# Turning the feed-forward rows by transposing transfers, widened by ScalarE, in place of TensorE transposes

## The reference, cut to what matters

```python
def _rmsnorm(x, g):
    return g * (x * rsqrt(mean(x * x, -1) + EPS))
def _act_quant(x):
    scale = 127.0 / clip(max(abs(x), -1), 0.0001)
    return clip(round(x * scale), -128, 127) / scale
def _linear_bit(x, w, g):
    return einsum('bsd,od->bso', _act_quant(_rmsnorm(x, g)), _ternary_quant(w))
h = silu(_linear_bit(x, w1, g1)) * _linear_bit(x, w2, g2)      # 512 -> 2048
ffn = _linear_bit(h, w3, g3)                                    # 2048 -> 512
...
x = x + tanh(g_xattn) * xattn(layernorm(x), ctx)
x = x + tanh(g_ffn) * ffn(layernorm(x))                         # x: 2 x 512 x 512
```

## Time and profile before

| what | value |
|---|---|
| time, median of 3 runs | 653.92 us (652.92 to 654.09) |
| the profiled execution's own time | 656.19 us |
| its span | 654.4 us |
| PE, DVE, ACT, POOL busy over the span | 97%, 82%, 65%, 55% |
| granted TensorE clock | full in every slice |
| the feed-forward steps t = 2 to 7 and the end | from about 570 us to the end |

### The profile page before, as it was taken

One profiled execution on the slowest core, in us unless ns is written; L12 is line 12 of the kernel. 1 busy time (PEld: TensorE's weight loads), 2 busy tenths in 40 slices (PEclk: granted clock), 3 DMA queues, 4 the chain that ended last, 5 costly groups with the idle time before them and its releaser, 6 DMA issues.

```text
span 654.4 us, 9986 instructions
## 1 busy us (share of the span) xinstructions
PE 635.1 (97%) x2968; PEld 394.0 (60%) x2968; DVE 536.5 (82%) x870; ACT 422.2 (65%) x693; POOL 360.2 (55%) x304
## 2 busy tenths in 40 slices
PE   8789999999999999999999999999999998999997
PEld 7555466766766676666666666566656554545553
DVE  4778787788878877887789978997899987998863
ACT  2564686477737764776567766776666633598875
POOL 4722376655545554565367854664457144686651
PEclk9999999999999999999999999999999999999999
DMA  8207976788589858984988798878689872000001
GB/s 283 87 6 188 274 196 164 206 223 240 151 227 241 219 131 239 251 224 106 251 222 221 201 242 224 222 195 231 169 221 251 198 177 81 1 1 33 17 35 48
DMA packets 45208, 112.79 MB, mean 172 GB/s; under 512 B 11888, under 2 KB 15088, under 8 KB 45040
## 3 DMA queue, kind: packets, MB, share of 16 engines
q1 hardware_dynamic: 42128, 104.24, 60.1%
q10 hardware_dynamic: 2976, 8.06, 4.0%
q0 software_dynamic: 64, 0.00, 0.0%
HBM read 45.16 MB, written 2.10 MB: 72 GB/s over the span
## 4 chain that ended last, share of the span: by engine, by line
PE 68%; DVE 10%; SPq 8%; ACT 4%; issue 4%; DMA 3%; POOL 1%; PEld 1%; POOLq 0%; ACTq 0%; DVEq 0%; PEldq 0%
PE ps_s L1443 11%; SPq L1132 8%; PE ps_b L1476 6%; PE ps_s L623 5%; PE ps_ctx L1476 5%; PE ps_b L1339 4%; PE ps_b L1394 4%; DMA G<-E 3%; PE ps_b L1341 3%; PE ps_b L1413 3%; PE ps_b L1340 3%; ACT E L1675 2%; PE ps_b L674 2%; DVE small L1858 2%; PE ps_ctx L1472 2%
## 5 line engine op out<-in xcount | busy, mean ns | idle before, releaser
L1675 ACT ACTIVATE E<-ps_s,small 128x1024 f32<-128x1024 f32 x128 | 142.5, 1116 | 143.4 <-DVE small L1858 110.5
L1241 POOL TENSOR_TENSOR G_lo<-G,g_hi 128x512 fp32r<-128x512 f32 x130 | 168.0, 1306 | 117.7 <-ACT g_hi L1619 117.7
L1858 DVE TENSOR_REDUCE small<-ps_s 128x1 f32<-128x1024 f32 x128 | 149.8, 1211 | 34.5 <-PE ps_s L1443 34.3
L1872 DVE STREAM_TRANSPOSE E<-E 128x1024 f32<-128x1024 f32 x124 | 152.0, 1230 | 0.1
L1199 POOL TENSOR_SCALAR E<-E,small 128x1024 f32<-128x1024 f32 x64 | 78.9, 1233 | 109.6 <-DVE small L1864 98.0
L1619 ACT ACTIVATE g_hi<-G 128x512 fp32r<-128x512 f32 x130 | 76.9, 631 | 3.5 <-DVE wq L1888 3.5
L1339 PE MATMUL ps_b<-b_hi,ctx_hi 128*128 128x512 f32 x128 | 66.8, 522 | 0.3 <-DVE ctx_lo L1818 0.3
L1476 PE MATMUL ps_b<-G,kv 128*128 128x512 f32 x126 | 63.7, 600 | 1.7 <-DMA G<-E 1.7
L1476 PE MATMUL ps_ctx<-G,kv 128*128 128x512 f32 x126 | 64.6, 607 | 0.1
L1443 PE MATMUL ps_s<-k_hi,q_hi 64*128 64x512 f32 x256 | 57.3, 444 | 3.8 <-ACT E L1675 2.6
L623 PE MATMUL ps_s<-wq,q12T 128*128 128x512 fp8e4 x256 | 59.8, 379 | 0.1
(11 more groups left out here) (203 smaller groups left out, 1211.7 us busy)
## 6 DMA issues: line engine op xcount, KB each, us to landing
G<-E SPq DMA_DIRECT2D x496, 128.0 KB, 2.6
w_stage<-in_wffn SPq DMA_DIRECT2D x37, 512.0 KB, 4.8
w_stage<-in_wffn ACTq DMA_DIRECT2D x11, 512.0 KB, 4.4
wo_s<-in_woT SPq DMA_DIRECT2D x8, 512.0 KB, 5.4
wq_s<-in_wq SPq DMA_DIRECT2D x7, 512.0 KB, 5.5
wkcq_s<-in_wkcqT SPq DMA_DIRECT2D x7, 384.0 KB, 3.4
out<-x_sb SPq DMA_DIRECT2D x8, 256.0 KB, 2.0
x_sb<-in_x SPq DMA_DIRECT2D x3, 512.0 KB, 6.3
```

The source lines that it names most:

```text
L1241: nc.gpsimd.tensor_tensor(g_tile(w % 2, i, G_lo), tile, high_part(i).bitcast(F32).rearrange("p (t i q) -> p t i q", t=ST, i=4), ALU.subtra ...
L1675: nc.scalar.activation(out, scores, ACT.Exp, bias=negmax[:, k:k + 1], accum_out=rowsum[:, k:k + 1]).then_inc(exp_done, 1)
L1858: nc.vector.tensor_reduce(negmax[:, k:k + 1], ps_s[:, t % 2, :], AX_X, ALU.max, negate=True).then_inc(max_done, 1)
L1872: nc.vector.transpose(e_tile(w % 2, t), e_tile(w % 2, t)).then_inc(blocks_turned, 1)
```

## The change

For the normed rows of tiles 2 to 7 and the hidden rows of tiles 0 to 5, TensorE's transposes and ScalarE's copies out of PSUM go. In their place ScalarE rewrites the rounded int16 rows as bf16 in the same bytes (`widen_rows`, 128 x 1024, and `widen_hidden`, 128 x 2048), and SP issues a transfer that turns them from SBUF to SBUF (`dma_start_transpose`), one for each. The first two tiles' rows and the last two tiles' hidden rows are turned by TensorE as before. Every wait on the old copies now waits for the transfer.

```diff
-        T3_AT = (1, 2)
+        FIRST_MOVED, LAST_MOVED = 2, 5
...
+            def turn_rows(t):
+                sp.wait_ge(q12_wide, t - FIRST_MOVED + 1)
+                sp.wait_ge(up_done, HC * (t - 1))
+                sp.dma_start_transpose(q12T[:, t % 2, :, :, :].rearrange("p i c s -> p (i c) s"),
+                                       qn12[:, t % 2, :, :].rearrange("p i d -> p (i d)").bitcast(BF16)).then_inc(q12_moved[t % 2], 16)
+
+            def turn_hidden(t):
+                sp.wait_ge(q3_wide, t + 1)
+                if t >= 2:
+                    sp.wait_ge(mm3_done, t - 1)
+                sp.dma_start_transpose(q3T[:, t % 2, :, :], qn3[:, t % 2, :].bitcast(BF16)).then_inc(q3_moved[t % 2], 16)
+
+            for t in range(1, TT):
+                if t + 1 < TT:
+                    turn_rows(t + 1)
+                if t >= 2:
+                    turn_hidden(t - 2)
+                if t >= 3:
+                    store(t - 3)
+            for t in range(LAST_MOVED, TT):
+                store(t)
...
         def gate_up(pe, t, k, c):
-            pe.wait_ge(q12T_ready, 2 if early and c == 1 else t + 1)
+            if t < FIRST_MOVED:
+                pe.wait_ge(q12T_ready, 2 if early and c == 1 else t + 1)
+            else:
+                pe.wait_ge(q12_moved[t % 2], 16 * (t // 2))
...
                     if out and not (isinstance(t, int) and t == LAST):
-                    pe.wait_ge(et_free, 2 * t + (ET_FREE0 - 2))
+                    pe.wait_ge(q3_moved[t % 2], 16 * (t // 2))
...
+        def widen_rows(act, t):
+            act.wait_ge(q12_ready, t + 1)
+            rows = qn12[:, t % 2, :, :].rearrange("p i d -> p (i d)")
+            copy_act(rows.bitcast(BF16), rows).then_inc(q12_wide, 1)
+
+        def widen_hidden(act, t):
+            act.wait_ge(q3_ready, t + 1)
+            rows = qn3[:, t % 2, :]
+            copy_act(rows.bitcast(BF16), rows).then_inc(q3_wide, 1)
...
                     if turn and c == 0:
-                        turned_rows(act, t, k)
-                    if out and c in T3_AT:
-                        a = T3_AT.index(c)
-                        act.wait_ge(t3_done, 2 * t + (a - 3))
-                        copy_act(q3T[:, k, 8 * a:8 * a + 8, :].rearrange("p c s -> p (c s)"), t3[:, a, :]).then_inc(et_free, 1)
+                        widen_rows(act, t + 1)
...
                 if t == 1:
                     silu(act, 2, 0, 0)
+                    widen_hidden(act, 0)
                     norm_act(act, 2, 0)
-                elif mm:
+                else:
+                    widen_hidden(act, t - 1)
                     hidden_square(act, t, k)
```

More of the change, by code:

```diff
@@ L464, in build @@
         atanh_pool, yg_first = sem("atanh_pool"), sem("yg_first")
+        q12_wide, q3_wide = sem("q12_wide"), sem("q3_wide")
+        q12_moved, q3_moved = [sem("q12_moved0"), sem("q12_moved1")], [sem("q3_moved0"), sem("q3_moved1")]
         mm3_done, side_read, stored, ffn_chain, atanh_dve, atanh_act, ln2_var, ln2_done, ln2_bias = (
@@ L528, in ffn_sp, with store @@
             sp.dma_start(g3, A["g3"].partition_broadcast(P)).then_inc(ld_g3, 16)
-            with sp.Fori(0, TT) as t:
+            def store(t):
                 sp.wait_ge(side_read, t + (SIDE_READ0 + 1))
-                sp.dma_start(out_dram[:, bass.ds(t, 1), :], x_sb[:, bass.ds(t, 1), :]).then_inc(stored, 16)
+                sp.dma_start(out_dram[:, t:t + 1, :], x_sb[:, t:t + 1, :]).then_inc(stored, 16)
+            def turn_rows(t):
[17 more added lines that the diff above has]
+                store(t)
             sp.wait_ge(stored, 16 * TT)
@@ L615, in gate_up @@
             cols = slice(c * NF, (c + 1) * NF)
-            early = isinstance(t, int) and t == 0
-            pe.wait_ge(q12T_ready, 2 if early and c == 1 else t + 1)
+            early = t == 0
+            if t < FIRST_MOVED:
+                pe.wait_ge(q12T_ready, 2 if early and c == 1 else t + 1)
+            else:
+                pe.wait_ge(q12_moved[t % 2], 16 * (t // 2))
             if not (early and c < 2):
@@ L658, in step @@
                             pe_last_out(pe, s)
-                    if turn and c == 0:
-                        turn_rows(pe, t, k)
-                    if out and c in T3_AT:
-                        a = T3_AT.index(c)
[L663 to L668, removed]
                 if out and not (isinstance(t, int) and t == LAST):
-                    pe.wait_ge(et_free, 2 * t + (ET_FREE0 - 2))
+                    pe.wait_ge(q3_moved[t % 2], 16 * (t // 2))
                     pe.wait_ge(side_read, t + (SIDE_READ0 - 2))
@@ L680, in turn_half @@
                 pe.wait_ge(q3_half, 2 * (t - (LAST - 1)) + a + 1)
-                pe.wait_ge(et_free, 2 * t + (a - 1 + ET_FREE0))
+                pe.wait_ge(et_free, ET_FREE0 + (a + 1 if t == LAST else 0))
                 for b in range(8):
@@ L687, in down_half @@
             def down_half(t, a):
-                pe.wait_ge(et_free, 2 * t + (a + 1 + ET_FREE0))
+                if t <= LAST_MOVED:
+                    pe.wait_ge(q3_moved[t % 2], 16 * (t // 2 + 1))
+                else:
+                    pe.wait_ge(et_free, 2 * (t - LAST_MOVED - 1) + (a + 1 + ET_FREE0))
                 if a == 0 and t < LAST - 1:
@@ L790, in step @@
                 if quant:
-                    if not (isinstance(t, int) and t < 3):
-                        act.wait_ge(t3_done, 2 * t - 4)
+                    if t >= 3:
+                        act.wait_ge(q3_moved[(t - 3) % 2], 16 * ((t - 3) // 2 + 1))
                     act.wait_ge(hfac_chain, HCH * t)
@@ L812, in round_part @@
                 if a == 0:
-                    act.wait_ge(t3_done, 2 * t - 2)
+                    act.wait_ge(q3_moved[t % 2], 16 * (t // 2))
                     act.wait_ge(hfac_chain, HCH * (t + 1))
@@ L817, in copy_half @@
             def copy_half(t, a):
-                act.wait_ge(t3_done, 2 * t + (a + 1))
+                act.wait_ge(t3_done, 2 * (t - LAST_MOVED - 1) + (a + 1))
                 copy_act(q3T[:, t % 2, 8 * a:8 * a + 8, :].rearrange("p c s -> p (c s)"), t3[:, a, :]).then_inc(et_free, 1)
@@ L932, in norm_quant @@
             scales(dve, y_am[:, 2 * k:2 * k + 2], fs[:, bass.ds(t + 10, 1)], y_fac[:, 2 * k:2 * k + 2], yfac_chain, 3 * t + 6)
-            if not (isinstance(t, int) and t < 0):
+            if 0 <= t < FIRST_MOVED:
                 dve.wait_ge(t12_done, t + 1)
+            elif t >= FIRST_MOVED:
+                dve.wait_ge(q12_moved[t % 2], 16 * (t // 2))
             for i in range(2):
```

## The result

The changed kernel takes **658.46 us** (median of 5 runs, 657.84 to 660.17) against 654.09 us (652.92 to 655.05, 5 runs) of the kernel before, measured side by side: ratio 1.0064, 95% interval 1.0048 to 1.008. It is 4.4 us slower. The forecast was slower by 13 (667.0, range 655.5 to 690): the sign and the range held, the size did not.

The account below looks back on a forecast made before the run. The prediction took TensorE to bound the feed-forward steps at 11.7 us, with a loop without it at 11.59 close behind. Terms of +4.8, +9.7 and -1.3 made +13.2 us, added to the median: 667 us, range 655.5 to 690.

Parts of the forecast that it names:

- 11.59 us loop without TensorE: Feed-forward steps: root to root through GpSimd, VectorE and ScalarE; free transposes would shorten steps 3 to 5 only 0.11 us each.
- ScalarE's widening in the loop: Steps 3 to 5: 1.83 us of widening between rounding and square makes the loop 12.0 us against 11.59.
- The transfer loop is 6.3 + L: Step length from down products through silu, widening and both transfers to the next down products; hidden up to L = 5.4.
- L: Time from the end of the rows' widening to the hidden rows' landing; 4.6 to 9.7 us, taken as 8.0.
- The dear reading: Transfer price by 256-byte pieces, 2.7 ns each and 1.3 us fixed; 1024 + 2048 pieces give L = 9.7.
- the first term: First down products: they wait for the widenings and the transfers, ending at 583.5 against 578.67, +4.8 us.
- (2): From first to fifth down products: four steps of 14.3 us, 57.2 against 47.5, +9.7 us.
- Rival 1: Feed-forward steps: transfers hidden with L under 5.4, ScalarE's widening pays; +2.1 us, 656; chance 0.17.
- (3), the end: Last step and end: two transposes on TensorE and ScalarE's copies with them go, -1.3 us.
- Rival 2: Feed-forward transfers slower still, from smaller pieces or slow issuing; L = 13 as a mark, +38 us, 692; chance 0.14.
- Rival 3: TensorE's clock falls to 1.2 GHz behind each wait in the steps; +22 us on top, 689; chance 0.07.
- Rival 4: Feed-forward steps: not slower, if widening takes 0.9 us at double rate and L is under 5.4; 653; chance 0.05.

Follow-up runs that it names:

- e3: Changed kernel with hidden rows written as bf16 at once, without rounding to whole numbers or widening, and their transfer issued ahead of the rows': 651.85 us.
- e4: Changed kernel with each rows' transfer issued a second time into an unread buffer, ahead of the hidden rows' transfer: 665.30 us.
- e6: Against the changed kernel, only hidden tiles 0 to 5 are turned by transfers; TensorE turns the rows: 657.04 us.
- e8: Against the changed kernel, only row tile 7 and hidden tiles 4 and 5 are turned by transfers, hidden rows first: 652.94 us.
- e5: Against the changed kernel, only row tiles 2 to 7 are turned by transfers; hidden tiles go back to TensorE: 653.64 us.
- e7: Changed kernel with ScalarE widening the hidden rows behind silu 0 of the next step and their transfer issued ahead of the rows': 654.57 us.

## Why the prediction was right in its mechanism and wrong in its size

- **The 11.59 us loop without TensorE, 0.11 us to gain in a step.** Right. With both new costs taken out (e3) the steps are 11.55 to 11.57 us, and the kernel gains 3.0 us in all, not the 8 that six steps of 1.35 us would give. (The step before these, 11.84 us, had a fall of the clock in it.)
- **ScalarE's widening in the loop: 12.0 us.** Right: 12.12. The widenings took 1.04 and 1.91 us (1.03 and 1.91 forecast), 1.81 to the next instruction (1.83). The 0.12 over are in the rounding, 2.03 to the next start instead of 1.90: the widening, which comes next, waits for the semaphore that the rounding raises (`q3_ready`), as the square behind it before did not.
- **The transfer loop is 6.3 + L.** Right: 12.1 at L = 5.8, and one more issue of 1.33 us made it 13.4 to 13.8 (e4).
- **The failed step: "I take 8.0, nearer to the dear end".** L was 5.8: 1.25 us in which SP issues the rows' transfer, 0.1, and 4.4 from the hidden rows' issue to the landing. The dear reading had the size of the pieces right and their price wrong. There are 30704 - 11888 = 18816 more packets under 512 bytes, as 6 x 3072 = 18432 pieces of 256 bytes would be. But 1024 pieces land in 3.2 us and 2048 in 4.4: by an estimate from these two 1.2 ns a piece and 2.0 us fixed, where `wkr_s` and `wqr_s` gave 2.7 and 1.3. And the two don't queue behind each other but for SP's issue: alone the hidden rows land in 4.3 us (e6), behind the rows in 4.4. I had counted one transfer's pieces behind the other's. With 5.8 for 8.0 the first term is 575.4 + 5.8 + 0.1 - 578.67 = +2.6, as measured, and the whole sum would have been 2.6 + 0.9 - 1.3 = +2.2 instead of +13.2. The rest, up to the measured +4.4, is the next point.
- **A term missing in (2).** With L = 5.8 the four steps of 12.1 give 48.4 - 47.5 = +0.9, but +3.0 was measured: the first of them took 14.26 us. I put all four at one length. That first step is not yet in the loop, and it had 12.41 us before: the two widenings of hidden tiles 0 and 1 (1.81 us each) stand ahead of its square on ScalarE, which so starts 2.9 us later behind the last `ctx_lo` than before (25.07 against 22.16), and the widening of the rows, SP's issue and the landing follow behind that. Rival 1 had this as "pushes the square by 1.83"; the main sum left it out. With hidden tiles alone (e6), where no down product waits for a transfer, that square starts 25.22 us behind the last `ctx_lo`, so ScalarE is late without the two transfers in a row as well. The second down products come 33.10 us behind it in e6, 35.20 in the changed kernel and 30.77 before: 2.3 of the 4.4 us go with ScalarE's delay, and the other 2.1 with the wait for the transfer. The lines of e6, then that of the kernel before:

```profile
557.70 0.68 DVE L1930 TENSOR_TENSOR ctx_lo<-ps_b,ctx_hi 128x512 fp32r<-128x512 f32 x1
...
582.92 1.90 ACT L824 ACTIVATE junk_h<-h_f 128x2048 f32<-128x2048 f32 x1
...
590.80 3.62 PE L744 MATMUL ps_b<-wq,q3T 128*128 128x512 fp8e4 x16
```

```profile
591.08 3.62 PE L674 MATMUL ps_b<-wq,q3T 128*128 128x512 fp8e4 x16
```

- **(3), the end.** -1.4 against -1.3. That the late part pays is shown by e8, which keeps the change only in step 6 and the end and gains 1.5 us. The place isn't shown as reckoned: in e8's profiled execution 0.7 us of the gain stand ahead of the fifth down products and 0.6 behind them.
- **Rival 1** (hidden transfers, 656) named half of what happened; alone it is e6, +2.7 against its +2.1. Its condition, L under 5.4, was missed by 0.4 us. That the kernel got slower at all did not hang on L: the widening alone is enough for that, and the wide range held with a wrong L. **Rival 2** didn't occur. **Rival 3**: the clock did fall, once in the profiled execution (mean 0.997), and cost nothing there; the two executions at 0.995 took 659.9 and 660.2 us, the three at 0.997 and 1.0 took 657.8 to 658.5. **Rival 4** failed on both conditions: the widening took 1.81 us and L was 5.8.
- **"TensorE idle about 4 us five times"**: five times, but 1.5 to 2.5 us. "Steps 14.3 apart": 12.1; that the first stood 14.26 apart is chance, since it came about by the term that was missing.

The Trainium skill, "Advanced Engine Details and Errata", X-Bar Transpose (TRN2), has these transfers as fast as ordinary ones. For 512 KB the trace agrees (4.4 us, where `w_stage` took 4.8); for 256 KB it took 3.2, where the store took 2.0. Neither of these two ordinary ones goes from SBUF to SBUF. By the two landings 256 KB more took 1.2 us, an estimated 218 GB/s, below the 350 to 400 that the prediction quotes. That rule would have brought me nearer than my own reading, at L = 4, but to the wrong side: it says nothing of the 1.25 us of issuing that stand ahead here, and with them the transfers are not hidden.

## What to carry to other kernels

Before work is taken off the engine that bounds, follow the loop of the others: here it stood 0.11 us behind, so the change could pay only outside the steps where that loop is closed, and a gain that stays was shown for the last steps alone. Price a transfer that someone waits for as issue time on its queue, plus a fixed landing, plus pieces, and keep the cheap and the dear reading apart until a row decides; what matters is also what stands ahead on the queue: the same extra transfer cost 6 to 7 us ahead of the wanted one and nothing that can be told behind it. When two loops tie, cutting one shows only a part (here the loss went from 4.4 us to 3.2 or 2.1, and with both cut to a gain of 3.0): cut both before saying what a loop costs.

## What the runs showed of the hardware that was not expected

In the steps of the changed kernel SP takes 1.23 to 1.25 us to issue a transposing transfer of 256 KB and 1.6 to 3.0 us for one of 512 KB, and what stands behind it on the queue waits for that. An ordinary store of 256 KB took 0.35 to 0.56 us behind the rows' transfer alone (e5), and 0.71 to 1.30 directly behind the hidden rows' transfer in the changed kernel. So the issue time depends on what was issued just before: directly behind the hidden rows' transfer the one of 256 KB took 1.60 to 1.98 us (e7).

TensorE's granted clock fell behind single waits. In the changed kernel, behind the 2.49 us at the first down products, in the view of stretches (the column ahead of the last two is the clock):

```profile
578.00:582.00 4.00, 3.16 (x8) 1.19 (x9) 3.75 (x14) 2.85 (x2) 3.56 (x4) 0.57 0.02 6
```

A mean of 0.57 is mostly the lower level, 1.2 GHz; the 16 products took 5.08 us instead of 3.61. It cost nothing, since ScalarE, which the next steps hang on, did not wait for these products. With the hidden rows first it fell behind a wait of 3.98 us for the product of chunk 0, in the loop:

```profile
587.86 6.20 PE L690 MATMUL ps_s<-wq,q12T 128*128 128x512 fp8e4 x16 [3.98 <-issue]
```

and the roots there stood 13.98 us apart, where hidden tiles alone had 12.11 with the clock full. The later waits of the changed kernel (1.5 to 2.1 us) were followed by a full clock, and in e4 so were waits of 2.9 to 3.3 us; behind waits of 2.61 us (e3) and 2.69 us (e7) it fell, and sixteen products took 5.30 us in both. In e7 ten executions with a mean clock of 0.999 or 1.0 took 653.6 to 655.7 us, and two at 0.997 took 656.9 and 658.9; in e4 the three at 0.997 took 663.9 to 664.9, two at 0.994 665.7 and 666.5, one at 0.989 670.0. So a fall costs some 2 us where it meets the loop. The Trainium skill, "TensorE: Matmul & The Clock Gate", Part 1, has an idle array fall to the lower level; the trace agrees for the waits of 2.49 and 3.98 us, while others of like length had no such fall behind them. Which wait is followed by a fall in which execution stays open.
